# New issue orders for four engines in the input expert stage and the first ten projections of one kernel

## What is computed

```python
x = x + 0.5 * ffn(layernorm(x), router_weight, router_bias, expert_bias)
x = x + attn(layernorm(x), Wq, Wk, Wv, Wo, Wg, Win, dt_bias, A_log_bias, gnorm_w)
x = x + 0.5 * ffn(layernorm(x), router_weight, router_bias, expert_bias)

def ffn(h):                       # flat h: [2048, 512], 64 experts, top 8
    scores = softmax(h @ router_weight.T + router_bias)
    w = top 8 of scores           # the rest is zero
    return h * w.sum(-1) + w @ expert_bias

def attn(h):                      # 32 query heads, 8 key/value heads, chunks of 128 tokens
    q, k, v = rope(h @ Wq.T), rope(h @ Wk.T), h @ Wv.T
    dt = softplus(h @ Win.T + dt_bias); g = -dt * exp(A_log_bias)
    G = cumsum(g) within a chunk; x = v * dt
    y = (q k^T * exp(G_i - G_j) for i >= j) x + exp(G) q state
    state = state * exp(G_last) + (k * exp(G_last - G))^T x
    return (rmsnorm(y) * gnorm_w * silu(h @ Wg.T)) @ Wo.T
```

## Time and profile before

| what | value |
|---|---|
| median of 3 runs | 1737.37 us (1737.26 to 1737.95) |
| the profiled execution's own time | 1738.0 us |
| its span, first to last instruction | 1736.2 us |
| busy: PE, DVE, ACT, POOL | 1669.2, 1419.3, 1119.1, 1224.6 us |
| mean granted clock of PE, of full speed | 0.983 |

### The profile page before, as it was taken

The page is one execution under the profiler, slowest core; times in us unless marked ns, Lnnn a source line. Parts: engine busy times, 40 slices in busy tenths (PEclk is TensorE's granted clock), DMA queues, the critical chain, the costliest instruction groups (busy, mean ns, idle before and its releaser), DMA issues. The chain is left out here.

```text
span 1736.2 us, 34997 instructions
## 1 busy us (share of the span) xinstructions
PE 1669.2 (96%) x11668; PEld 954.9 (55%) x11668; DVE 1419.3 (82%) x3109; ACT 1119.1 (64%) x3011; POOL 1224.6 (71%) x1188
## 2 busy tenths in 40 slices
PE   6778999999999999999999999999999999999986
PEld 5534555555555555555555555555555555555554
DVE  7768788787887878788887888788897888788887
ACT  4546666666766666666676666666676666666652
POOL 4537677776877777776877777776777767777754
PEclk8889999999999999999999999999999999999998
DMA  5011102110111102110111101110111101110002
GB/s 210 2 46 34 38 19 73 38 44 25 44 62 31 38 19 68 44 44 25 44 56 38 37 19 56 49 49 21 44 60 38 37 19 56 49 38 19 26 13 98
DMA packets 39058, 76.90 MB, mean 44 GB/s; under 512 B 4832, under 2 KB 5856, under 8 KB 37856
## 3 DMA queue, kind: packets, MB, share of 16 engines
q1 hardware_dynamic: 38880, 74.66, 13.2%
HBM read 70.19 MB, written 4.46 MB: 43 GB/s over the span
## 5 line engine op out<-in xcount | busy, mean ns | idle before, releaser
L1370 POOL TENSOR_TENSOR PL<-PF,PH 128x512 bf16<-128x512 f32 x128 | 158.2, 1236 | 305.7 <-ACT PH L1129 305.7
L337 PE MATMUL B<-WH,XTH 128*128 128x512 bf16 (+1 forms) x1024 | 282.5, 300 | 8.7 <-POOL WL L1328 5.8
L339 PE MATMUL B<-WH,XTL 128*128 128x512 bf16 (+1 forms) x1024 | 282.5, 300 | 0.0
L338 PE MATMUL B<-WL,XTH 128*128 128x512 bf16 (+1 forms) x1024 | 282.5, 300 | 0.0
L1129 ACT ACTIVATE PH<-PF 128x512 bf16<-128x512 f32 x128 | 80.9, 632 | 278.7 <-DVE PF L1560 278.7
L337 PE MATMUL B<-XTH,WH 128*128 128x512 bf16 x640 | 244.4, 382 | 3.3 <-DVE QF L1526 3.3
L339 PE MATMUL B<-XTH,WL 128*128 128x512 bf16 x640 | 244.5, 382 | 0.0
L338 PE MATMUL B<-XTL,WH 128*128 128x512 bf16 x640 | 244.4, 382 | 0.0
L1335 POOL TENSOR_TENSOR QS<-QS,SIN 128x512 f32<-128x512 f32 x160 | 204.5, 1278 | 50.2 <-ACT QS L1085 50.2
L1610 DVE SCALAR_TENSOR_TENSOR YF<-B,RR,G 128x128 f32<-128x128 f32 x512 | 143.9, 344 | 71.0 <-POOL RR L1377 70.9
L337 PE MATMUL B<-WH,ZTH 128*128 128x512 bf16 x512 | 194.0, 379 | 2.3 <-POOL WL L1328 1.7
(11 more groups left out here) (198 smaller groups left out, 4469.0 us busy)
## 6 DMA issues: line engine op xcount, KB each, us to landing
ROWS<-rows_dram SPq DMA_DIRECT2D x128, 256.0 KB, 3.3
STAGE<-in_wall SPq DMA_DIRECT2D x108, 256.0 KB, 2.8
ACC<-in_x SPq DMA_DIRECT2D x3, 1024.0 KB, 10.2
out<-ACC SPq DMA_DIRECT2D x3, 1024.0 KB, 4.0
ACC<-in_x SPq DMA_DIRECT2D x4, 256.0 KB, 3.2
COS<-in_cos SPq DMA_DIRECT2D x1, 1024.0 KB, 13.0
SIN<-in_sin SPq DMA_DIRECT2D x1, 1024.0 KB, 15.6
out<-ACC SPq DMA_DIRECT2D x4, 256.0 KB, 2.1
```

The lines of the kernel that those rows point to most:

```text
L337: nc.tensor.matmul(out_, ah, bh, start=first, stop=False)
L338: nc.tensor.matmul(out_, ah, bl, start=False, stop=False)
L339: return nc.tensor.matmul(out_, al, bh, start=False, stop=last)
L1370: nc.gpsimd.tensor_tensor(PL[:, n % 2, :], PF[:, :], PH[:, n % 2, :], ALU.subtract).then_inc(pl_ready.sem, 1)
```

## The change

It writes the four lists of calls anew, from the first transposes to the start of the main loop, and T_ORDER with them. No operation is added or taken out, and SP's list stays as it is. Six helpers (pe_mix, pool_residual, dve_mixed, pe_turn2, act_turned2, dve_turned2) get an argument `chunks`, as others had already, so that a block's four calls can stand apart. What the new lists do, beside the finer weave: a block's logits are made chunk by chunk between the transposes, and those of blocks 2 and 3 before or among the mixes of the blocks before them; block 0's dt comes before the first fill; fills 3 to 7 stand before pe_dt(2), pe_sums(0) and the second transposes of block 3; scores(0, 0) stands before the last fill, and decayed(0, 0) before keys_lo and the last two gates. POOL splits the weight pieces one by one (1, 0, 2, 4, 3, 6, 5, 8, 7, 9).

```diff
-T_ORDER = ([("turn", 0, i) for i in range(BLK)] + [("turn", 1, i) for i in range(BLK)] + [("turn", 2, i) for i in range(BLK)]
-           + [("second", 0, i) for i in range(BLK)] + [("dt", 0, 0)] + [("turn", 3, i) for i in range(BLK)]
...
+T_PARTS = (("turn", 0, 0, 4), ("turn", 1, 0, 4), ("turn", 2, 0, 4), ("second", 0, 0, 4), ("turn", 3, 0, 2), ("dt", 0, 0, 1), ("turn", 3, 2,
+           2), ("second", 1, 0, 4), ("dt", 1, 0, 1), ("second", 2, 0, 4), ("dt", 2, 0, 1), ("second", 3, 0, 4), ("dt", 3, 0, 1))
+T_ORDER = [(kind, f, first + i) for kind, f, first, count in T_PARTS for i in range(count)]
...
-        def pe_mix(pe, f):
+        def pe_mix(pe, f, chunks=range(BLK)):
...
-            for i in range(BLK):
+            for i in chunks:
...
```

PE:

```diff
+pe_turn(pe, 0, (0, 1))
+pe.wait_ge(ones_ready.sem, 1)
+pe_centre(pe)
+pe_turn(pe, 0, (2,))
+pe_logits(pe, 0, (0,))
+pe_turn(pe, 0, (3,))
+pe_logits(pe, 0, (1, 2, 3))
+pe_turn(pe, 1, (0, 1))
+pe_weights(pe, 0)
+pe_turn(pe, 1, (2,))
+pe_mix(pe, 0, (0, 1))
+pe_logits(pe, 1, (2, 1))
+pe_mix(pe, 0, (2, 3))
+pe_turn(pe, 1, (3,))
+pe_logits(pe, 1, (0,))
+pe_turn(pe, 2, (0,))
+pe_logits(pe, 1, (3,))
+pe_turn(pe, 2, (1, 2, 3))
+pe_weights(pe, 1)
+pe_turn2(pe, 0, (0,))
+pe_mix(pe, 1, (0, 1))
+pe_turn2(pe, 0, (1,))
+pe_mix(pe, 1, (2,))
+pe_turn2(pe, 0, (2,))
+pe_mix(pe, 1, (3,))
+pe_turn2(pe, 0, (3,))
+pe_logits(pe, 2, (2, 1, 0))
+pe_turn(pe, 3, (0,))
+pe_logits(pe, 2, (3,))
+pe_turn(pe, 3, (1,))
+pe_dt(pe, 0)
+pe.wait_ge(f_xtl.sem, f_xtl.at(0, BLK - 1))
+fill(0, 0, 0, None, True, 0)
+pe_turn(pe, 3, (2, 3))
+pe_weights(pe, 2)
+pe_turn2(pe, 1, (0,))
+pe_logits(pe, 3, (0,))
+pe_mix(pe, 2, (0, 1))
+pe_logits(pe, 3, (2,))
+pe_mix(pe, 2, (2,))
+pe_turn2(pe, 1, (1,))
+pe_logits(pe, 3, (1,))
+pe_mix(pe, 2, (3,))
+pe_logits(pe, 3, (3,))
+fill(0, 0, 1, None, True, 0)
+pe_turn2(pe, 1, (2,))
+fill(0, 0, 2, None, True, 0)
+pe_weights(pe, 3)
+pe_turn2(pe, 1, (3,))
+pe_mix(pe, 3, (0, 1))
+pe_dt(pe, 1)
+fill(0, 0, 3, None, True, 0)
+pe_mix(pe, 3, (2, 3))
+fill(0, 0, 4, None, True, 0)
+fill(0, 0, 5, None, True, 0)
+pe_turn2(pe, 2)
+fill(0, 0, 6, None, True, 0)
+fill(0, 0, 7, None, True, 0)
+pe_dt(pe, 2)
+pe_turn2(pe, 3, (0,))
 pe_sums(pe, 0)
+pe_turn2(pe, 3, (1,))
 pe_rows(pe, 0)
+pe_turn2(pe, 3, (2, 3))
+pe_sums(pe, 1)
+turn_keys(0, 0)
+pe_dt(pe, 3)
 fill(0, 0, 8, None, True, 0)
+pe.wait_ge(d_in.sem, d_in.at(NB - 1, 0))
+scores(0, 0)
 fill(0, 0, 9, None, True, 0)
 pe_rows(pe, 1)
```

ACT, after act_turned(act, 0) and the copies EBH and WINH:

```diff
 act_exp(act, 0)
 act_weights(act, 0)
+act_turned(act, 1, (0, 1, 2))
+split_hi(0, 0)
+split_hi(0, 1)
+act_turned(act, 1, (3,))
+act_turned(act, 2, (0,))
 act_exp(act, 1)
+act_normalise(act, 0, (0,))
+act_turned(act, 2, (1,))
+act_normalise(act, 0, (1,))
 act_weights(act, 1)
+act_turned(act, 2, (2,))
+act_normalise(act, 0, (2,))
+act_turned(act, 2, (3,))
+act_turned2(act, 0, (0, 1))
+act_normalise(act, 0, (3,))
+act_turned2(act, 0, (2, 3))
+split_hi(0, 2)
+split_hi(0, 3)
+nc.scalar.activation(ALOG[:, :], ALOG[:, :], ACT.Exp).then_inc(a_ready.sem, 1)
+split_hi(0, 4)
+act_turned(act, 3, (0,))
+split_hi(0, 5)
+act_turned(act, 3, (1,))
+split_hi(0, 6)
 act_exp(act, 2)
+act_normalise(act, 1, (0,))
+act_turned(act, 3, (2,))
+act_weights(act, 2)
+act_turned2(act, 1, (0,))
+act_normalise(act, 1, (1,))
+act_turned(act, 3, (3,))
+act_normalise(act, 1, (2,))
+split_hi(0, 7)
 swap(0, 0, 0, 0)
+act_turned2(act, 1, (1,))
 act_exp(act, 3)
+split_hi(0, 8)
+act_normalise(act, 1, (3,))
 swap(0, 0, 1, 1)
+act_turned2(act, 1, (2,))
 act_weights(act, 3)
+act_turned2(act, 1, (3,))
+swap(0, 0, 2, 2)
+swap(0, 0, 3, 3)
+act_normalise(act, 2, (0,))
+hi(0, 0, 0)
+act_normalise(act, 2, (1,))
+act_dt_exp(act, 0)
+swap(0, 0, 4, 4)
 act_normalise(act, 2, (2, 3))
+split_hi(0, 9)
 act_turned2(act, 2)
 hi(0, 0, 1)
 hi(0, 0, 2)
+values(0, 0, 5)
+gate(0, 0, 0, 6)
+act_normalise(act, 3)
+gate(0, 0, 1, 7)
+act_turned2(act, 3, (0,))
+act_sums(act, 0)
+act_turned2(act, 3, (1,))
+act_rows(act, 0)
 hi(0, 0, 3)
+act_turned2(act, 3, (2, 3))
 hi(0, 0, 4)
+act_dt_exp(act, 1)
 gate(0, 0, 2, 8)
+decay(0, 0)
 act_sums(act, 1)
+keys_hi(0, 0)
+p_hi(0, 0)
 gate(0, 0, 3, 9)
 wv_hi(0, 0)
 decay(0, 1)
+act_rows(act, 1)
```

POOL:

```diff
 pool_rstd(pool, 0, 0)
 pool.wait_ge(const_act.sem, 2)
 nc.gpsimd.tensor_tensor(FIRST.EBL[:, :], FIRST.EBF[:, :], FIRST.EBH[:, :], ALU.subtract).then_inc(lows_ready.sem, 1)
+pool_scales(pool, 0)
 nc.gpsimd.tensor_tensor(WINL[:, :, :], WINF[:, :, :], WINH[:, :, :], ALU.subtract).then_inc(lows_ready.sem, 1)
 pool_residual(pool, 0)
+split_lo(0, 1)
 pool_rstd(pool, 0, 1)
 pool_rstd(pool, 1, 0)
 pool_scales(pool, 1)
 pool_residual(pool, 1)
+pool_rstd(pool, 0, 2)
+split_lo(0, 0)
+split_lo(0, 2)
+split_lo(0, 4)
+split_lo(0, 3)
 pool_rstd(pool, 1, 1)
 pool_scales(pool, 2)
+pool_residual(pool, 2, (0,))
+split_lo(0, 6)
+pool_residual(pool, 2, (1, 2))
+pool_rstd(pool, 0, 3)
+pool_residual(pool, 2, (3,))
 pool.wait_ge(rope_landed.sem, 32)
 times_sin(0, 0, 0)
+split_lo(0, 5)
+pool_scales(pool, 3)
+times_sin(0, 0, 1)
+pool_residual(pool, 3)
+times_sin(0, 0, 2)
 pool_rstd(pool, 1, 2)
+split_lo(0, 8)
+split_lo(0, 7)
 times_sin(0, 0, 3)
+times_sin(0, 0, 4)
 pool_rstd(pool, 1, 3)
+split_lo(0, 9)
 pool.wait_ge(after_ready.sem, 1)
 pool_wj(pool, 0)
+lo(0, 0, 0)
+lo(0, 0, 3)
+lo(0, 0, 4)
 mask_rows(0, 0)
+mask_rows(0, 1)
 pool_wj(pool, 1)
 pool.wait_ge(d_wj.sem, d_wj.at(1, 0))
 weighted_v(0, 0)
+p_lo(0, 0)
 wv_lo(0, 0)
```

DVE:

```diff
+dve_stats(dve, 0, 0, (0, 1))
+dve_centre(dve)
+dve_stats(dve, 0, 0, (2, 3))
+dve_logits(dve, 0)
+dve_choose(dve, 0)
+dve_stats(dve, 0, 1, (0,))
+dve_weigh(dve, 0)
+dve_stats(dve, 0, 1, (1, 2, 3))
+dve_mixed(dve, 0, (0, 1))
+dve_stats(dve, 1, 0, (0, 1))
+dve_stats(dve, 0, 2, (0,))
+dve_mixed(dve, 0, (2, 3))
+dve_stats(dve, 1, 0, (2, 3))
+dve_logits(dve, 1)
+dve_choose(dve, 1)
+dve_stats(dve, 0, 2, (1,))
+dve_weigh(dve, 1)
+dve_stats(dve, 0, 2, (2, 3))
+dve_mixed(dve, 1, (0, 1))
+dve_stats(dve, 0, 3, (0,))
+dve_turned2(dve, 0, (0, 1))
+dve_stats(dve, 1, 1, (0, 1))
+dve_turned2(dve, 0, (2,))
+dve_mixed(dve, 1, (2,))
+dve_turned2(dve, 0, (3,))
+dve_stats(dve, 1, 1, (2,))
+dve_mixed(dve, 1, (3,))
+dve_logits(dve, 2)
+dve_stats(dve, 1, 1, (3,))
+dve_choose(dve, 2)
+dve_dt_in(dve, 0)
+dve_weigh(dve, 2)
+dve_stats(dve, 0, 3, (1, 2, 3))
+dve_mixed(dve, 2, (0,))
+dve_turned2(dve, 1, (0,))
+dve_mixed(dve, 2, (1,))
+dve_stats(dve, 1, 2, (0, 1))
+times_cos(0, 0, 0, 0)
+dve_mixed(dve, 2, (2,))
+dve_logits(dve, 3)
+dve_mixed(dve, 2, (3,))
+dve_stats(dve, 1, 2, (2,))
+dve_choose(dve, 3)
+dve_stats(dve, 1, 2, (3,))
+dve_weigh(dve, 3)
+add_sin(0, 0, 0, 0)
+dve_turned2(dve, 1, (1, 2, 3))
+times_cos(0, 0, 1, 1)
+times_cos(0, 0, 2, 2)
+dve_mixed(dve, 3, (0, 1))
+dve_stats(dve, 1, 3, (0,))
+dve_dt_in(dve, 1)
+dve_stats(dve, 1, 3, (1,))
+dve_dt_abs(dve, 0)
+add_sin(0, 0, 1, 1)
+add_sin(0, 0, 2, 2)
+dve_mixed(dve, 3, (2, 3))
 times_cos(0, 0, 3, 3)
+dve_stats(dve, 1, 3, (2, 3))
+dve_series(dve, 0, 0)
+dve_turned2(dve, 2)
+times_cos(0, 0, 4, 4)
 dve_series(dve, 0, 1)
+dve.wait_ge(c_landed.sem, 16 * 6)
+nc.vector.tensor_scalar(AFTER[:, :], TRIF, -FAR, FAR, ALU.mult, ALU.add).then_inc(after_ready.sem, 1)
 dve_series(dve, 0, 2)
 dve_series(dve, 0, 3)
 add_sin(0, 0, 3, 3)
+add_sin(0, 0, 4, 4)
+dve_dt_in(dve, 2)
+dve_turned2(dve, 3, (0,))
+v_lo(0, 0, 5)
+silu2(0, 0, 0, 6)
+dve_turned2(dve, 3, (1, 2, 3))
+silu2(0, 0, 1, 7)
+dve_dt_in(dve, 3)
 q_lo(0, 0, 1)
+dve_dt_abs(dve, 1)
 q_lo(0, 0, 2)
+dve_series(dve, 1, 0)
+decayed(0, 0)
+nc.vector.tensor_scalar(GNH[:, :], GN[:, :], 0.5, None, ALU.mult).then_inc(const_dve.sem, 1)
+keys_lo(0, 0)
 silu2(0, 0, 2, 8)
 silu2(0, 0, 3, 9)
```

217 lines of the change are left out of this document (37 added, 180 removed).

## The result

The changed kernel takes 1710.29 us (median of 4 runs, 1709.83 to 1710.96) beside 1737.66 for the kernel before on the same chip (4 runs, 1737.26 to 1739.55): a ratio of 0.9837, 95% interval 0.9825 to 0.9848, 27.4 us less. On a second chip it took 1708.39 us (5 runs) beside 1740.08, a ratio of 0.9822 (0.9809 to 0.9836). The forecast was 1717.4 with a range from 1710.4: the sign and the place were right, the size was not, and the first median lies just outside the near end.

A forecast was written before the change was run, and what follows sets the result against it. PE bounds the main loop; ahead of it DVE's holes of order cost time. The walk's 28.5 us less 5 and 3 gave 20.5, rounded to 20 off 1738.0; the median, 0.6 lower, 1717.4 us, range 1710.4 to 1727.4.

The forecast's parts named there:

- What the walk leaves out: Deductions from the walk's 28.5 us: 5 for hops and clock, 3 for POOL beside DVE, the loop unchanged.
- hops and clock: Engine-to-engine hops and PE's half clock along DVE's chain before the loop: 5 us off the gain, ends 2 and 9.
- POOL beside DVE: Before the loop, DVE operations stretched where they meet POOL's SBUF work: 3 us off the gain, ends 0 and 8.
- the loop carried through unchanged: At the main loop's entry, the gain passes through unchanged, with 1 us either way.
- the walk: Hand timing of the new lists before the loop, one clock per engine, at trace pitches: gain 28.5 us at first state's matmul.
- The bound: DVE's work from 12.66 us is 86.4 us, so decayed scores end no earlier than 99.1; at most 27 us gain.
- POOL did not become the bound: Rival: POOL's long operations stretch before the loop and POOL becomes the bound; gain 10, 1727.4 us; chance 0.14.
- The walk exact: Rival: the hand timing before the loop holds as it stands; gain 27 to 28, 1709.4 us; chance 0.05.
- The row chain: Rival: SP's row send waits for POOL's late piece 9, delaying the first mask; slower, 1742.0 us; chance 0.03.

The follow-up runs named there:

- port_read: Changed kernel plus six spare POOL subtractions that read SBUF, in POOL's hole from 80.4 to 89 us beside DVE's series; 1717.90 us.
- new_control: The changed kernel unaltered, measured again on a second chip; 1708.39 us (5 runs).
- p_dve: Changed kernel plus four spare statistics (2.46 us) on DVE near 50 us, ahead of block 3's statistics; 1711.04 us (one run).
- before_warm: Kernel before the change plus 32 idle-time matmuls on PE; 1738.12 us (10 runs), ratio 0.9994 to the kernel before.
- tail_undo: Changed kernel with scores(0, 0), p_hi and decayed(0, 0) put back behind the last gates; 1710.84 us (one run).
- early_undo: Changed kernel with DVE's first statistics of blocks 1 and 2 and block 0's mixes and second statistics whole calls again; 1710.58 us (one run).
- mid_fills: Changed kernel with fills 3 to 7 behind pe_turn2(2) and pe_dt(2) again, swaps 3 and 4 and times_cos(3) behind turned2(2); 1720.42 us, ratio 0.9884.
- row_late: Changed kernel with two spare 1.8 us memsets on POOL once the rows have landed, ahead of the first mask; 1714.26 us (one run).
- both_undo: Changed kernel with the edits of mid_fills and block 3's logits whole again behind block 1's second transposes; 1723.64 us, ratio 0.9908.

## Why the prediction missed

**The step that failed** is "What the walk leaves out": 5 us for hops and clock, 3 for POOL beside DVE, and the loop carried through unchanged. The 28.5 us of the walk are its gain at the first state's matmul. There the gain was 25.5, 3.0 less in place of 8. From there to ZTL 4 and the end it grew by 2.6 us, where I had put nothing, within 1. 28.5 - 3.0 + 2.6 = 28.1, beside the 20.5 of my sum.

At the decayed scores, where DVE's own account can be made, the walk had 98.2 and they ended at 99.50, 1.3 later. DVE started at 11.93 in place of 12.66 (0.7 earlier), had 4.7 us of holes that the walk hardly has, and was busy for 82.8 us where the walk gives it 98.2 - 12.66 = 85.5 (2.7 less): 98.2 - 0.7 + 4.7 - 2.7 = 99.5.

- **Hops and clock.** The holes of 4.7 us are the 5 that I took. As a size it was right.
- **POOL beside DVE.** I added 3 us. DVE's operations that meet POOL cost over their undisturbed length: before, 2.0 in the add_sins (4 x (1184 - 682) ns), 0.9 in dt_abs and 1.1 in WJ, 4.0 in all; after, 0.7 in FNM (0.90 for 0.17), 0.9 in WJ (1.20 for 0.28), 1.1 in DT (1.36 for 0.28) and 0.3 in dt_abs (0.68 for 0.42), 3.0 in all. The meetings became fewer: I had counted those of the new list and forgotten that the old rows, and the bound made of them, already held more. The sign of the term was wrong. That a meeting can cost 0.9 and more is right (port_read); that the new lists would have more of them was assumed from "the same work in less time".
- **The bound.** 84.4 + 3.8 - 1.8 = 86.4 held the old meetings, and three things more. The rows give 3.7 and not 3.8 (129.76 - 126.06), and 0.7 of it is one more meeting (the DCH operation behind the old decayed scores took 1.15 us in place of 0.42). And DVE's records overlap where operations stand back to back (a length of 0.68 at a pitch of 0.60), which the busy time of a window doesn't count twice: the 235 records before sum to 97.6 us and the 237 after to 97.5 (count times mean, group by group), but the windows show 84.4 and 82.8. The list without holes is shorter by 1.5 us of overlap more. With the measured 82.8 the bound was 12.66 + 82.8 = 95.5 us and not 99.1, and "at most 27 us are to be had" was wrong as a limit. It is why I gave a gain above 27 so small a chance.

**The way to the first state.** From the decayed scores to its matmul it is 6.7 us in the profile after and 5.2 in new_control and p_dve, whose fill runs at full clock; the walk had 5.1. So 1.5 of the 3.0 us missing there are the half clock of that fill.

**The loop's entry.** From the decayed scores to ZTL 2 it was 38.6 us before and is 36.5 now, in the profile after and in twelve of the fourteen others that edit it or repeat it, at either clock of the fill, so 2.1 us of gain come here (28.7 at ZTL 2). before_warm, whose fill ran at full clock, took 37.9, so up to 0.7 of the 2.1 may be the clock's. The other 1.4 stand at the second decayed scores, which start 4.5 us behind the first ones now (98.39 to 102.91) and 6.0 before (124.93 to 130.89, and as long in before_warm), released by ACT's PF in both. Which move did that is not shown. The gates and keys_lo didn't: tail_undo has them ahead of the decayed scores again and takes 36.5 us too. Then 0.9 us were lost again up to ZTL 4 in the profile after, at a clock of 0.78 in the 14 us ahead of ZTL 3, and 0.0 in the profiles with 0.88 or 1.00 (early_undo lost 0.3 at 0.88).

**What was right.** The bound was DVE and its holes, and the holes were of order. The low halves ended at 33.0, 48.3 and 62.7 us (walk 31.2, 47.3, 61.0; forecast near 32, 49, 64). Scores(0, 0) at 94.96 (walk 93.8; the forecast's 97 to 104 missed). The row send at 89.55 (walk 87.1, forecast near 92). The first state's matmul at 106.2 (walk 103.9 for its end, forecast near 112, within its 104 to 122). "Fill 3 stood behind pe_turn2(2) and pe_dt(2), which held PE for those 6.0 us" is the dearest single sentence of the walk: mid_fills puts 8 to 13 us on it.

**The rivals.** POOL did not become the bound: it is busy 19.3 of 25 us from 50 to 75, and no sine ahead of the scores takes over 1.28 us. "The walk exact", given one chance in twenty, was nearest (1709.4), but by luck in part: its gain at the decayed scores was 1.3 us too high and at the first state 3.0, and the loop's entry made up for it. The row chain did not slow the kernel, but row_late shows it 0.4 us from being the last, where I had given it 1.2.

What stays open: how the gain behind mid_fills splits. both_undo still gains 15.9 us, the early weave and the tail cost nothing that single runs could tell, and so most of the rest should lie in the fills against pe_sums and pe_turn2(3), in POOL's order, or in parts that cover for one another. These weren't taken apart.

## What to carry to other kernels

Walk a new order by hand with the pitches of the trace, and take off only what a row of the trace says is missing from it: here the walk was 1.3 us off at the decayed scores and 3.0 at the first state, and the general caution took off 8. Before a term for contention is added, count the same contention in the rows that the prices came from; a new order may remove more of it than it brings. A busy-time bound from a trace full of holes is too high, by the stretched operations and by the overlaps that it lacks. And look for the call that holds a whole engine for the input of a later stage (here pe_turn2(2) and pe_dt(2) ahead of five fills): it was the dearest of the groups taken back, and the early weave taken back alone cost nothing that showed.

## What the runs showed of the hardware

- The same program got a granted clock of 0.50 or 0.96 from 20 to 26 us, with PE busy for all 6 us in both (26 against 50 matmuls); the low half of block 2 came 2.1 us earlier for it, the decayed scores 0.5.
- A DVE TENSOR_SCALAR on 128x256 f32 took 1.87 us beside a POOL memset that only writes, and 0.28 without; two-input operations beside such a memset kept their 0.41 to 0.42 us. Beside POOL subtractions that read SBUF, three two-input operations took 4.21 us in place of 1.35.
- The fill of 12 matmuls behind the decayed scores took 4.1 us at a pitch of 0.43 us for its first seven and 2.6 at 0.22, and the second ZTL came 36.5 us behind the decayed scores in both cases. A granted clock of 0.78 in place of 0.88 or 1.00 ahead of the third ZTL went with 0.9 us more up to the fourth.
